# A four-layer attention kernel on one core: the last four gating steps and the first projections woven into the FFN's iterations, and the FFN's normalisation moved from GpSimd to VectorE

## What is computed

```python
# L0: quantised-weight attention over ctx, 16 heads of 8
x = x + attend(layer_norm(x) @ Wq, ctx @ Wk, ctx @ Wv) @ Wo
# L1: self attention, cross attention, FFN, a layer norm after each
x = layer_norm(x + mha(x, x))
x = layer_norm(x + mha(x, ctx))
x = layer_norm(x + gelu(x @ ff_w1 + b1) @ ff_w2 + b2)
# L2: gating by a pooled vision vector per batch
vision = mean(ctx) @ Wv + bv
text = x @ Wt + bt
coupling = 2 * sum(text * vision)
r = softmax(coupling over the 64 tokens) * vision
x = layer_norm(x + sigmoid(text @ Wg_t + r @ Wg_v + bg) * r)
# L3: grouped-query attention with rotary tables, then a gated MLP, both residual
h, kv = rmsnorm(x), rmsnorm(ctx)
x = x + softmax(rope(h @ Wq) @ rope(kv @ Wk).T + mask) @ (kv @ Wv) @ Wo
x = x + (silu(rmsnorm(x) @ Wgate) * (rmsnorm(x) @ Wup)) @ Wdown
```

## Time and profile before

| | us |
|---|---|
| median of 3 runs (lowest to highest) | 585.86 (583.68 to 589.11) |
| the profiled execution | 585.07, its span 583.3 |
| busy: PE, DVE, ACT, POOL | 506.8, 404.7, 316.9, 251.8 |
| mean granted TensorE clock | 0.977 of full |
| FFN, from `mlp_in(0)` to the last residual sum | 229.13 to 271.7 |
| round -1, up to the start of `scores3(0)` | 271.7 to 301.65 |

### The profile page before, as it was taken

One profiled execution on the slowest core, in us unless ns is written; L12 is line 12 of the kernel. 1 busy time (PEld: TensorE's weight loads), 2 busy tenths in 40 slices (PEclk: granted clock), 3 DMA queues, 4 the chain that ended last, 5 costly groups with the idle time before them and its releaser, 6 DMA issues.

```text
span 583.3 us, 14128 instructions
## 1 busy us (share of the span) xinstructions
PE 506.8 (87%) x5446; PEld 404.7 (69%) x5446; DVE 404.7 (69%) x1005; ACT 316.9 (54%) x761; POOL 251.8 (43%) x281
## 2 busy tenths in 40 slices
PE   0699999879999996895669699899999999998985
PEld 0367887657777775784547477788787878776874
DVE  4368866788777775256487979787878987784522
ACT  1177887647777776475242636455564636344331
POOL 4645633478788787889310313132222223112110
PEclk9999999989999999999678999999999999999998
DMA  9920000000000000000000000000000000000000
GB/s 295 269 111 3 2 3 3 2 3 1 3 4 2 3 3 1 1 1 2 0 1 0 2 1 0 1 1 11 2 10 1 1 11 1 9 2 10 1 10 18
DMA packets 12121, 11.75 MB, mean 20 GB/s; under 512 B 5144, under 2 KB 10136, under 8 KB 11928
## 3 DMA queue, kind: packets, MB, share of 16 engines
q1 hardware_dynamic: 11624, 9.54, 5.9%
q10 hardware_dynamic: 432, 1.32, 0.6%
HBM read 9.81 MB, written 1.05 MB: 19 GB/s over the span
## 4 chain that ended last, share of the span: by engine, by line
PE 51%; DVE 26%; issue 10%; POOL 7%; ACT 5%; DMA 1%; POOLq 0%; DVEq 0%; ACTq 0%
PE ps L436 7%; DVE wide L1225 5%; PE ps L450 4%; PE ps L426 4%; PE ps L418 4%; PE ps L574 4%; DVE wide L1230 3%; PE ps L588 3%; PE ps L610 3%; DVE mx L1286 2%; PE ps L664 2%; PE ps L379 2%; DVE p L1288 2%; PE ps L461 2%; PE ps L380 2%
## 5 line engine op out<-in xcount | busy, mean ns | idle before, releaser
L1446 POOL TENSOR_TENSOR probs<-p,rc 128x512 f32<-128x512 f32 x32 | 33.7, 1054 | 155.9 <-DVE rc L1297 155.9
L1057 DVE TENSOR_REDUCE negm<-ps 128x8 bf16<-128x512 f32 x96 | 59.6, 682 | 24.8 <-PE ps L418 24.8
L911 ACT ACTIVATE p<-p 128x512 f32<-128x512 f32 x32 | 20.2, 631 | 101.2 <-DVE p L1288 101.2
L574 PE MATMUL ps<-shared,wq 128*128 128x256 f32 x256 | 68.7, 396 | 4.6 <-DVE w L1256 2.3
L765 ACT ACTIVATE shared<-ps 128x512 f32<-128x512 f32 x96 | 57.4, 600 | 24.3 <-PE ps L436 22.6
L1408 POOL TENSOR_TENSOR wide<-wide,cv 128x1024 f32<-128x1024 f32 x24 | 49.3, 2053 | 48.4 <-DVE wide L1036 48.4
L1353 POOL TENSOR_TENSOR rstd<-veps,neghalf 128x2 f32<-128x2 f32 x40 | 29.1, 728 | 74.6 <-DVE veps L1081 47.5
L1225 DVE TENSOR_TENSOR wide<-ps,cst 128x512 f32<-128x512 f32 x64 | 43.2, 675 | 25.4 <-PE ps L574 25.4
L436 PE MATMUL ps<-cst,p 128*128 128x128 f32 x384 | 59.2, 278 | 0.4 <-ACT shared L765 0.4
L759 ACT ACTIVATE p<-ps 128x512 f32<-128x512 f32 x96 | 54.5, 596 | 7.4 <-PE ps L426 7.3
L574 PEld LDWEIGHTS ps<-shared,wq 128*128 128x128 f32 x256 | 46.6, 195 | 15.5 <-DVE w L1256 4.3
(11 more groups left out here) (180 smaller groups left out, 1173.3 us busy)
## 6 DMA issues: line engine op xcount, KB each, us to landing
late<-in_mask_l SPq DMA_DIRECT2D x2, 512.0 KB, 8.7
wq<-in_wq SPq DMA_DIRECT2D x1, 1024.0 KB, 8.6
result<-x_all SPq DMA_DIRECT2D x8, 128.0 KB, 1.8
x_all<-in_x_tok SPq DMA_DIRECT2D x1, 896.0 KB, 9.9
wide<-in_ctx_t SPq DMA_DIRECT2D x1, 896.0 KB, 11.6
rv<-in_rv ACTq DMA_DIRECT2D x1, 768.0 KB, 7.4
cst<-in_cst ACTq DMA_DIRECT2D x1, 512.0 KB, 4.8
wa<-in_wa SPq DMA_DIRECT2D x1, 512.0 KB, 9.5
```

The lines of the kernel that those rows point to most:

```text
L574: ins = mm(bank_of(f"q{i}", g)[:, j * GT:j * GT + GT], wq3[:, 2 * i + j, :], hn_t[:, g % 2, 0:GT], start=True, stop=True, skip_group_check ...
L1057: V.tensor_reduce(negm[:, n % 4, :], ps[:, S_BANK[r], :].rearrange("p (a k) -> p a k", k=S), AX.X, ALU.max, negate=True).then_inc(sm["dve_ ...
```

## The change

`EARLY` holds all twelve steps of rounds -3 to -1 instead of eight: round -3 is pulled together (its steps 1 and 2 both run in iteration 3), round -2 runs in iterations 5 and 6, round -1 in 7 and 8. The loops after the FFN begin a round later. `NEARLY` becomes the number of fills in these rounds, 23, so that the whole of round -1 goes round in two banks. `ld_w3` and `vz` are waited for ahead of the FFN instead of behind it. In the FFN, DVE normalises the two tiles after POOL's inverse root; POOL keeps root, scale and shift, and does `f_res(g+2)` between the root and the scale.

```diff
-        EARLY = {2: ((-3, 0),), 3: ((-3, 1),), 4: ((-3, 2),), 5: ((-3, 3),), 6: ((-2, 0),), 7: ((-2, 1),), 8: ((-2, 2), (-2, 3))}
-        NEARLY = 7
+        EARLY = {2: ((-3, 0),), 3: ((-3, 1), (-3, 2)), 4: ((-3, 3),), 5: ((-2, 0), (-2, 1)), 6: ((-2, 2), (-2, 3)),
+                 7: ((-1, 0), (-1, 1)), 8: ((-1, 2), (-1, 3))}
...
+        NEARLY = sum(len(step(r, u)) for r in ROUNDS[:3] for u in range(GB))
...
             pe.wait_ge(sm["ld_w"], 48)
+            pe.wait_ge(sm["ld_w3"], LD_W3)
             pe.wait_ge(sm["v_mean"], 1)
...
             pe.wait_ge(sm["m3_split"], 1)
-            pe.wait_ge(sm["ld_w3"], LD_W3)
-            for r in ROUNDS[2:]:
+            for r in ROUNDS[3:]:
...
+            act.wait_ge(sm["vz"], 1)
             act.wait_ge(sm["v_sum"], 1)
             A_(vmean[:, :], vpool[:, :], ACT.Copy, scale=1.0 / S).then_inc(sm["v_mean"], 1)
...
-            act.wait_ge(sm["vz"], 1)
-            for r in ROUNDS[2:]:
+            for r in ROUNDS[3:]:
...
                 dve.wait_ge(sm["f_y"], g + 1)
                 layer_norm(lambda t: y[:, gs, t, :], g, "f_", gs)
+                dve.wait_ge(sm["f_r"], g + 1)
+                for t in range(TG):
+                    ins = V.tensor_scalar(yg[:, gs, t, :], y[:, gs, t, :], mv[:, gs, t, 0:1], rstd[:, gs, t:t + 1],
+                                          ALU.subtract, ALU.mult)
+                ins.then_inc(sm["f_yn"], 1)
...
             for g in range(NG):
-                affine(sm["f_ve"], sm["f_r"], sm["f_yn"], sm["f_yg"], sm["f_x"], g, g, g % 2, "g3", "be3")
+                pool.wait_ge(sm["f_ve"], g + 1)
+                rsqrt(rstd[:, g % 2, :], veps[:, g % 2, :], TG, sm["f_r"])
                 if g + 2 < NG:
                     f_res(g + 2)
+                scale_shift(sm["f_yn"], sm["f_yg"], sm["f_x"], g, g, g % 2, "g3", "be3", yg, yg)
```

## The result

The changed kernel takes 600.99 us (median of 4 executions, 597.11 to 603.23) against 587.29 us (583.68 to 589.11) for the kernel before: ratio 1.0239, 95% interval 1.0197 to 1.028. I had forecast 589.5 and a range up to 595. The sign was that of the forecast, the size more than three times as large, outside the range.

A forecast was written before the change was run, and what follows sets the result against it. It took POOL to bound the FFN and DVE round -1, with PE idle 9.45 us between. Terms 6.2 + 0.9 - 8.8 + 3.6 + 2.1 + 0 = +4.0 gave 589.5 us, range 582 to 595.

The forecast's parts named there:

- Step 1: Start of the FFN: vmean waits for DVE's second clear, delaying mlp_in(0) by 6.2 us, plus 0.9 for cold products.
- The clock's term: At the start, mlp_up(0) runs at half clock after PE's idle gap, partly covered: +0.9 us, bounds 0 and 2.5.
- Step 2: FFN until hn(0) is ready: POOL no longer behind, so hn(0) at 272.9 instead of 281.7, -8.8 us.
- Step 4: Clock inside round -1: PE's gaps there lower the clock, +2.1 us, between 0 and +4.6.
- Step 3: From hn(0) to scores3(0): round -1's fills share engines with the last two FFN iterations, 23.5 instead of 19.9, +3.6 us.
- The term of the ring: Round -1 in two banks: a fill's wait each at q0 and q6, 0.4 us; otherwise DVE's sum covers PE's fill.
- Step 5: DVE/POOL port contention: 0, bounds 0 to 1.4 us; two added table loads at 1.28 each, already in the sums, without drain.
- Step 6: Behind scores3(0): round 0 begins as cold as before, 0 us, bounds 0 and -2.5.
- DVE's wait for the first q of round 0: Sign for the stages behind scores3(0): a wait near 4 or near 2 us would tell.
- cold through the early steps: Rival: PE's gaps keep 1.2 GHz from the first group on, +2.5 and +1.6 us, 593.6, say 594; chance 0.20.
- my own test: Decides the cold rival: it holds if the clock is low for over half of the last 20 us ahead of scores3(0).
- The rival of a warm hand-over: Gaps near the scores stay too short to matter: no clock loss in round -1, -2.5 us behind scores3(0), 585; chance 0.16.

The follow-up runs named there:

- e12: Changed kernel with 13 useless products ahead of PE's wait for v_mean and 27 in four gaps of the early steps, all waits kept: 595.3 us, ratio 1.0117.
- e5: The changed kernel once more, unaltered, as base for other runs on the same chip: 602.94 us, 1.0262 of the kernel before.
- e6: Changed kernel with 13 useless products on PE ahead of its wait for v_mean, wait kept: first distance 15.69 us instead of 20.07, medians differ by 6.2 us.
- e1: Changed kernel with ACT's wait for vz moved from ahead of vmean to ahead of the last early steps: 594.2 us, 1.0085 of the kernel before.
- e8: e1 plus useless products in PE's gaps, 7 ahead of mlp_up(5) and 20 in round -1: first y to first scores 64.07 us instead of 71.68.
- e9: Kernel before plus useless products only, in its gaps from the attention's end to the scores and ahead of l_text of group 3: 0.9916 of before.
- e10: Kernel before with the FFN's normalisation on DVE plus useless products in its gaps, 14 ahead of in: 0.9898 of before.
- e3: Kernel before with only the FFN's normalisation moved to DVE and f_res between root and scale: 586.9 us.
- e4: Kernel before with only the new order (EARLY, NEARLY, ROUNDS[3:]), normalisation on POOL, vz waited for late: +3.3 us by the medians.
- e7: e1 with round -1 behind the FFN again, in four banks, rounds -3 and -2 still packed: first y to first scores 67.04 us.
- e11: e8 plus the remaining useless products (ahead of q6, l_text of group 3, and single ones between attention and mlp_up(1)): 0.9958 of before.

## Why the prediction was wrong, step by step

The sum was +4.0, the spans differ by 18.1.

**Step 1, start: 7.1 forecast, 10.6 measured.** The wait was right, 6.2 against 6.3 (e12). ACT's row names it:

```profile
233.85 0.23 ACT L957 ACTIVATE vmean<-vpool 128x32 f32<-128x32 f32 x1 [6.53 <-DVE wide L1156]
```

The clock's term was mis-sized: 0.9 with an upper bound of 2.5, measured 4.4 (e5 against e6). I let only `mlp_up(0)` be cold and covered half of it. In fact the clock stayed at 0.5 for all of 236 to 246 us, `mlp_up(1)` included. In that time cold products and ACT took turns, each waiting for the other: ACT's Gelu waited for up in two halves, and up for `f_in`, so little was covered; why the clock did not return sooner no run shows. I had the row that warned of it: the old trace was cold for 9 us behind a shorter gap.

**Step 2, until `hn(0)`: -8.8 forecast, -3.1 measured.** The failing piece is the gap of 3.67 us ahead of `mlp_up(5)`. My own queue count had it: down(3) ends, and up(5) waits behind the exp and its two table loads. I gave it no clock, since step 4 looked for the clock in round -1 only: 2.9 us (e1 against e8). The other 2.8 show in e8, at full clock, set against my count on the same first y: `mlp_up(5)` starts 1.0 late, since ACT stands 0.77 us ahead of its exp for DVE's maximum (`agm`), which is queued behind the norm; y(5) starts 1.7 late, its norm ends 2.0 late and `l2_gate(1)` 2.9 late. The last us of it is `l2_gate(1)` beside a busy POOL: 284.61 to 286.96 in the changed kernel, 2.35 us instead of my 1.35. I had taken 1.35 from a group that ran beside an idle POOL; the old trace had `l2_gate(1)` itself, beside a busy one, at 2.68 us (272.96 to 275.64), most of it in one row:

```profile
273.95 1.69 DVE L1179 SCALAR_TENSOR_TENSOR gp<-ex,gvr,o_t 128x64 f32<-128x64 f32 x4
```

Timeline of DVE, changed kernel, with and without `f_res` on POOL at the same time:

```profile
283.68 1.00 DVE L1343 TENSOR_SCALAR yg<-y,mv,rstd 128x128 f32<-128x128 f32 x2 [0.82 <-POOL rstd L1359]
...
284.81 0.70 DVE L1174 TENSOR_TENSOR gvr<-exr,gv 128x4 f32<-128x4 f32 x1
...
285.62 1.34 DVE L1180 SCALAR_TENSOR_TENSOR gp<-ex,gvr,o_t 128x64 f32<-128x64 f32 x4
...
290.95 0.60 DVE L1343 TENSOR_SCALAR yg<-y,mv,rstd 128x128 f32<-128x128 f32 x2 [0.81 <-POOL rstd L1359]
```

Groups 0 to 5, which have an `f_res`, take 1.00 per pair of tiles, groups 6 and 7 0.60. The 0.60 of the earlier trace rows was right for the operation and wrong for its place. I had the cost bounded from 0 to 0.7 per group and took 0, on the ground that POOL's lighter load would give as much back. The Trainium skill (SBUF — State Buffer, "Who interferes with whom") puts it as "only the shared port pair causes contention, and it's an exclusive lock"; the row of 1.00 agrees in kind, while the wait is 0.4 and not the whole 0.7 of POOL's operation; the 128x4 operation at 284.81, 0.16 with POOL idle, took 0.70.

POOL's row of the changed kernel answers to the earlier trace rows; its next work waits for DVE now, not the other way round:

```profile
283.62 0.73 POOL L1444 TENSOR_TENSOR resb<-x_all,rv 128x256 f32<-128x256 f32 x1
284.77 0.72 POOL L1406 TENSOR_TENSOR yg<-yg,rv 128x256 f32<-128x256 f32 x1 [0.42 <-DVE yg L1343]
```

**Step 3, `hn(0)` to the scores: +3.6 forecast; at full clock +5.7** (25.68 in e8 and e12 less 19.94). The term of the ring was mis-sized. I counted 0.45 us for a q fill; it is four products and takes 1.13, start to start 0.87. At full clock DVE's sum and next read cover it while q follows q, but not where another fill stands between: in e8 DVE waits 0.77 ahead of q1, 1.03 ahead of q4 (behind `l_gate`) and 0.74 ahead of q6, 2.5 in all where I had 0.9, and its first q comes 0.4 later than I had it. The 19.94 that this step starts from held cold products of its own; against the filled old order (18.27 in e9, 18.99 in e10) the new one is 6.7 to 7.4 us longer. Timeline of DVE, e8:

```profile
282.99 0.69 DVE L1235 TENSOR_TENSOR wide<-ps,cst 128x512 f32<-128x512 f32 x1 [0.77 <-PE ps L582]
...
291.68 0.69 DVE L1235 TENSOR_TENSOR wide<-ps,cst 128x512 f32<-128x512 f32 x1 [1.03 <-PE ps L582]
...
298.08 0.69 DVE L1235 TENSOR_TENSOR wide<-ps,cst 128x512 f32<-128x512 f32 x1 [0.74 <-PE ps L582]
```

**Step 4, the clock in round -1: +2.1 forecast, 4.7 measured** (30.37 against 25.67), at my upper bound. The q fill again: cold it takes 1.9, longer than DVE's 1.07 per q, and with a ring of two PE stands at most two fills ahead. Timeline of DVE, changed kernel, two waits for cold products:

```profile
308.76 0.69 DVE L1226 TENSOR_TENSOR wide<-ps,cst 128x512 f32<-128x512 f32 x1 [3.20 <-PE ps L575]
...
311.56 0.42 DVE L1337 TENSOR_TENSOR y<-ps,resb 128x256 f32<-128x256 f32 x1 [1.12 <-PE ps L545]
```

**Step 5, table loads.** Six instead of four, each at 1.28. Where ACT waited for no other engine, the next activation stands right behind the load: 280.62 + 1.28 = 281.90, and the exp starts at 281.91. The drain of about 1.38 us that the Trainium skill (ScalarE: Activation LUTs, "What ACT_TABLE_LOAD costs") adds to each switch shows in no row here, so a sum with it would have been nearer to the result for a reason that isn't there.

```profile
280.62 1.28 ACT L823 ACT_TABLE_LOAD   x1
281.91 0.35 ACT L823 ACTIVATE ex<-o_t,agm 128x64 f32<-128x64 f32 x1
```

**Step 6, behind the scores: 0 forecast, -0.06 measured.** The number is right by luck. I had assumed scores as cold as before; they ran warm, the products of `scores3(0)` taking 1.09 instead of 1.98, and at the first reads of batches 0 to 29 the changed kernel is 1.05 to 1.8 us ahead of the old one, counted from the scores. DVE's wait for the first q of round 0, my sign for this step, was 3.90, near the old 4.15, and would have hidden it. The changed kernel loses 1.6 of its lead ahead of batch 30, behind a gap of some 2.9 us. The two executions have the same gap there and leave it at different clocks. Timeline of PE, changed kernel (granted clock 0.50 from 554 to 556 us):

```profile
553.17 0.66 PE L568 MATMUL ps<-cst,a_tok 128*128 128x128 f32 x2 [2.85 <-ACT a_tok L869]
...
554.48 1.91 PE L686 MATMUL ps<-probs_t,blocks 128*128 128x256 f32 x4
```

and the kernel before (1.00 from 530 to 540 us):

```profile
536.81 0.41 PE L567 MATMUL ps<-cst,a_tok 128*128 128x128 f32 x2 [2.86 <-ACT a_tok L868]
...
537.50 1.03 PE L685 MATMUL ps<-probs_t,blocks 128*128 128x256 f32 x4
```

Together: 3.5 (clock at the start), 2.9 (clock in the FFN), 2.8 (DVE beside POOL), 2.1 (fills at full clock), 2.6 (clock in round -1): 13.9 of the 14.1 us that were missing. Two thirds are clock. The error behind all three clock terms is one: I treated the clock as a small extra on a finished schedule, when in this stretch most gaps that the order makes are paid twice, once as a gap and once as slow products behind it. The rival "cold through the early steps" named the mechanism, with a chance of 0.20, and put 7.1 us of clock into the sum (3.0 of the forecast and 4.1 more); measured are 4.4 + 2.9 + 4.7 = 12.0. By my own test (a low clock for over half of the last 20 us ahead of the scores) it would have been denied: the mean there is 0.83, low for some 7 us. The test looked at one place for a loss that lay in four. The rival of a warm hand-over leaned on "no gap near the end over 2.5 us", though step 4 had counted one of 3.7 (2.83 in the run).

What was not separated: how much of the 2.8 us would go if DVE never met POOL (no run moved `f_res` away from the norm), and why the same gap leaves PE warm in one execution and cold in another.

## What to carry over

A wait that is moved up ahead of a chain costs its whole time if the chain feeds everything; ask where the signal is raised before moving it, here 6.5 us later than its new place, for buffers first filled at 312.9, almost 80 us on. When a schedule splits one long idle gap of PE into several of 3 to 6 us, price each of them with the products behind it at half clock as well, for as long as the nearest rows show it (here 6 to 10 us). A run with useless products in the gaps separates clock from order, but only if the kernel it is compared with gets them too: against the unfilled kernel the new order's loss in the stretch looked like clock alone, against the filled one 2.9 us of order came out.

## What the runs showed of the hardware

- After PE had idled 6.13 us the granted clock was 0.51 from 236 to 246 us although PE was listed busy for 8.62 of them; after 3.67 us it was 0.50 from 267 to 273 us; 13 products of no use in the first gap held it at 1.00 (e6).
- The length of a gap alone did not decide: after 2.86 us in the kernel before the clock stayed 1.00, after 2.85 us at the same place in the changed kernel it fell to 0.50; after 1.86 us it stayed 1.00 in the kernel before (244 to 248 us) and was 0.60 and 0.55 in e9.
- A DVE `tensor_scalar` on one 128x128 tile takes 0.34 us, and up to 0.75 beside POOL's `tensor_tensor` of SBUF tiles.
- The same stage can be entered warm or cold: 9.38 or 11.4 to 13.2 us for the same work (e8 against e1, e3, e4, e7). With fillers of 0.4 us in gaps of 0.4 to 1.0 us (e9 to e11) all three profiled executions had 9.37 or 9.38; as e8 had it without them, three are too few to show that the fillers did it.
